# Window attention and a sign convolution on one core: the residuals' biases move from TensorE to GpSimd, the last norm's scaling from VectorE to ScalarE

## The reference

```python
x  = norm(x + window_mha(x, x) + sa_bf)            # windows of 8x8 tokens, 8 heads of 16
lo = norm(avg4(x) + window_mha(avg4(x)) + sa_bf)   # 16x16 points, the same weights
x  = norm(x + window_mha(x, patches of lo) + ca_bf)
x2 = norm(x + relu(x @ w1 + b1) @ w2 + ffn_b2)     # 128 -> 512 -> 128
y  = batchnorm(conv3x3(sign(x2), sign(weight)))    # statistics over all images
out = x2 + y
```

## Time and profile before

| | |
|---|---|
| three runs | 2511.85, 2498.77, 2510.22 us; median 2510.22 |
| profiled execution | 2505.16 us |
| its span, first to last instruction | 2503.3 us |
| mean granted clock of PE | 0.945 |
| busy: PE | 2163.3 us (86%) |
| busy: DVE | 1595.5 us (64%) |
| busy: ACT | 1368.4 us (55%) |
| busy: POOL | 943.7 us (38%) |
| DMA | 393.57 MB, 157 GB/s on average |

### The profile page before, as it was taken

One profiled execution on the slowest core, in us unless ns is written; L12 is line 12 of the kernel. 1 busy time (PEld: TensorE's weight loads), 2 busy tenths in 40 slices (PEclk: granted clock), 3 DMA queues, 4 the chain that ended last, 5 costly groups with the idle time before them and its releaser, 6 DMA issues.

```text
span 2503.3 us, 93142 instructions
## 1 busy us (share of the span) xinstructions
PE 2163.3 (86%) x39704; PEld 1734.1 (69%) x39704; DVE 1595.5 (64%) x5098; ACT 1368.4 (55%) x2531; POOL 943.7 (38%) x1080
## 2 busy tenths in 40 slices
PE   6997889998899979999799997999889998898860
PEld 4775777776677757777577776777667776676730
DVE  4886766776566756677466665676656764555535
ACT  3664555665466645666356654566555554554535
POOL 3443443443344433444334433444334443333300
PEclk9999999999899989999899998999999999999985
DMA  6775655655456645555355554555455553434429
GB/s 173 210 201 157 189 154 150 167 168 149 117 163 170 169 119 153 167 166 159 98 165 155 163 158 124 166 168 155 137 142 162 167 146 107 132 117 116 138 78 394
DMA packets 335102, 393.57 MB, mean 157 GB/s; under 512 B 40033, under 2 KB 239458, under 8 KB 334690
## 3 DMA queue, kind: packets, MB, share of 16 engines
q1 hardware_dynamic: 333842, 386.62, 53.0%
q10 hardware_dynamic: 848, 0.99, 0.1%
HBM read 208.29 MB, written 160.27 MB: 147 GB/s over the span
## 4 chain that ended last, share of the span: by engine, by line
PE 59%; DVE 29%; ACT 5%; issue 4%; DMA 1%; POOL 1%; SPq 0%; POOLq 0%; DVEq 0%; ACTq 0%
PE ps_hid L714 9%; PE ps_y L725 9%; PE ps_proj L577 6%; PE ps_o L662 6%; DVE onorm L951 5%; PE ps_s L643 4%; PE ps_hid L744 3%; PE ps_s L649 3%; PE ps_t L675 3%; DVE negmax L939 3%; DVE xn L993 3%; PE ps_max L633 3%; PE ps_y L694 2%; PE ps_y L681 2%; DVE stats L980 2%
## 5 line engine op out<-in xcount | busy, mean ns | idle before, releaser
L1097 POOL TENSOR_TENSOR prob_lo<-prob,prob_hi 128x512 f16<-128x512 f32 x528 | 611.0, 1157 | 915.1 <-ACT prob_hi L812 915.1
L811 ACT ACTIVATE prob<-ps_s 128x512 f32<-128x512 f32 x528 | 313.8, 594 | 401.2 <-PE ps_s L649 395.7
L946 DVE RECIPROCAL rden<-ps_o 128x8 f32<-128x8 f32 x528 | 107.4, 203 | 523.6 <-PE ps_o L662 522.4
L939 DVE TENSOR_REDUCE negmax<-ps_max 128x8 bf16<-128x512 f32 x528 | 360.5, 683 | 118.1 <-PE ps_max L633 113.7
L951 DVE TENSOR_TENSOR onorm<-ps_o,rden 64x128 f32<-64x128 f32 x1056 | 304.5, 288 | 25.6
L812 ACT ACTIVATE prob_hi<-ps_s 128x512 f16<-128x512 f32 x528 | 313.2, 593 | 0.0
L662 PE MATMUL ps_o<-vb,prob_hi 128*128 128x68 f16 x4224 | 294.7, 197 | 3.0 <-DVE onorm L951 2.9
L725 PEld LDWEIGHTS ps_y<-w_sb,hid 128*128 128x128 f32 x2048 | 266.8, 196 | 31.7 <-issue 26.8
L714 PE MATMUL ps_hid<-xf,w_sb 128*128 128x512 f32 x512 | 286.1, 641 | 3.0 <-ACT yconv L869 2.1
L725 PE MATMUL ps_y<-w_sb,hid 128*128 128x128 f32 x2048 | 277.8, 280 | 0.6 <-ACT hid L850 0.6
L662 PEld LDWEIGHTS ps_o<-vb,prob_hi 128*128 128x128 f16 x4224 | 261.6, 100 | 9.6 <-issue 5.3
(11 more groups left out here) (116 smaller groups left out, 3557.9 us busy)
## 6 DMA issues: line engine op xcount, KB each, us to landing
k_rows<-k_flat SPq DMA_DIRECT2D x256, 256.0 KB, 3.2
qs<-q_rows SPq DMA_DIRECT2D x512, 128.0 KB, 3.2
ks<-k_rows SPq DMA_DIRECT2D x128, 512.0 KB, 4.7
q_rows<-q_flat SPq DMA_DIRECT2D x128, 256.0 KB, 2.4
vb<-v_flat SPq DMA_DIRECT2D x128, 136.0 KB, 4.2
vb<-values_out SPq DMA_DIRECT2D x128, 136.0 KB, 2.9
xin<-in_x SPq DMA_DIRECT2D x64, 256.0 KB, 3.1
self_out<-xa SPq DMA_DIRECT2D x64, 256.0 KB, 3.4
```

The costliest lines, as they stand in the source:

```text
L811: activation(prob[:, pair_no(u, k) % 2, :], ps_s[:, :], ACT.Exp)
L939: v.tensor_reduce(negmax[:, pair_no(u, k) % 2, :], ps_max[:, :].rearrange("p (a t) -> p a t", t=TOK), AX.X, ALU.max, negate=True).then_inc ...
L1097: g.tensor_tensor(prob_lo[:, i, :], prob[:, i, :], prob_hi[:, i, :], ALU.subtract).then_inc(s_prob, 1)
```

## The change

The matmul L683, its weight `ones2`, `brow` and their setup are gone. The biases come in as three more columns of `columns_sb`, one value per channel, that is, per partition. POOL adds them to the tokens before PE's residual transposes: `add_bias` in place to a unit's tokens, once all its projections have read them, and `add_bias2` from xf into a new tile, xf_plus. PE waits for each. `apply2` moves to ACT: in place of subtracting the mean and multiplying by 1/sqrt, it multiplies and adds a shift, -mean/sqrt, that POOL makes with two more small operations per strip. The new stages have the due times bias and bias2; those of apply2 and all others stay. In the diff, the first `apply2_to` is in ACT's block, the second in DVE's.

```diff
-            project=6.2, stats=6.5, rstd=6.55, apply=6.9, spread=7.56, spread_out=7.66, store=8.0, pool=8.6)
+            project=6.2, stats=6.5, rstd=6.55, apply=6.9, spread=7.56, spread_out=7.66, store=8.0, pool=8.6, bias=-4.7)
...
-             spread_out=7.36, h0=8.2, relu0=8.4, h1=9.2, relu1=9.4, resid2=9.45, f0=9.47, h2=10.2, relu2=10.4,
+             spread_out=7.36, bias=-4.6, bias2=7.75, h0=8.2, relu0=8.4, h1=9.2, relu1=9.4, resid2=9.45, f0=9.47, h2=10.2, relu2=10.4,
...
-           rstd=3.45, apply=3.8, spread=4.68, spread_out=4.76, pad=5.2, expand=5.7, kk0=6.85, kk0_hi=7.05,
+           rstd=3.45, apply=3.8, spread=4.68, spread_out=4.76, bias=-5.5, pad=5.2, expand=5.7, kk0=6.85, kk0_hi=7.05,
...
+        add_sb = columns_sb[:, 8 + FB:11 + FB]
-        ones2 = sb("ones2", [128, 128], F16)
-        brow = sb("brow", [128, 3, PAIRS, C], F16)
+        neg_mean2 = sb("neg_mean2", [128, PAIRS])
+        shift2 = sb("shift2", [128, PAIRS])
+        xf_plus = sb("xf_plus", [128, SW])
...
         def _(sp):
-            sp.dma_start(brow_f[:, :], bias_rows).then_inc(s_bias, 16)
-            def setup_bias():
...
-            setup_bias()
...
-            def residual(ps, pairs, src, bias):
+            def residual(ps, pairs, src):
                 for p in range(pairs):
-                    mm(ps[:, C * p:C * p + C], src[:, C * p:C * p + C], ident[:, :], is_transpose=True,
-                       start=(p == 0), stop=False, skip_group_check=True)
-                return mm(ps[:, 0:C * pairs], ones2[:, :], brow[:, bias, 0:pairs, :].rearrange("p a c -> p (a c)"),
-                          start=False, stop=False, skip_group_check=True)
+                    done = mm(ps[:, C * p:C * p + C], src[:, C * p:C * p + C], ident[:, :], is_transpose=True,
+                              start=(p == 0), stop=False, skip_group_check=True)
+                return done
...
-                residual(ps_y, u.pairs, tokens_of(u), which(u)).then_inc(s_resid, 1)
+                pe.wait_ge(s_plus, plus_no["bias", u.seq, None])
+                residual(ps_y, u.pairs, tokens_of(u)).then_inc(s_resid, 1)
...
-                residual(ps_y2, PAIRS, xf[:, u.no % 2, :], 2)
+                pe.wait_ge(s_plus2, u.no + 1)
+                residual(ps_y2, PAIRS, xf_plus).then_inc(s_resid2, 1)
...
-            pe.wait_ge(s_brow, 16 * 2 * PAIRS)
-            pe.wait_ge(s_prep_v, 4)
+            pe.wait_ge(s_prep_v, 1)
...
+            def apply2_to(u):
+                if u.no:
+                    act.wait_ge(s_t, out_turn[u.no - 1])
+                act.wait_ge(s_rstd2, u.no + 1)
+                for p in range(PAIRS):
+                    activation(xn2[:, C * p:C * p + C], ps_y2[:, C * p:C * p + C], ACT.Identity, bias=shift2[:, p:p + 1],
+                               scale=rstd2[:, p:p + 1]).then_inc(s_xn2, 1)
...
-            def apply2_to(u):
-                if u.no:
-                    dve.wait_ge(s_t, out_turn[u.no - 1])
-                dve.wait_ge(s_rstd2, u.no + 1)
-                for p in range(PAIRS):
-                    v.tensor_scalar(xn2[:, C * p:C * p + C], ps_y2[:, C * p:C * p + C], mv2[:, p, 0:1],
-                                    rstd2[:, p:p + 1], ALU.subtract, ALU.mult).then_inc(s_xn2, 1)
...
+            def root_and_shift(var, var_eps, to, neg_mean, to_shift, pairs, count, mv_done, var_done, root_done, rstd_done):
+                pool.wait_ge(mv_done, count)
+                g.tensor_tensor(var_eps[:, 0:pairs], var[:, 0:pairs, 1], eps[:, 0:pairs], ALU.add)
+                g.tensor_scalar(neg_mean[:, 0:pairs], var[:, 0:pairs, 0], -1.0, None, ALU.mult).then_inc(var_done, 1)
+                pool.wait_ge(var_done, count)
+                g.tensor_tensor(to[:, 0:pairs], var_eps[:, 0:pairs], half_neg[:, 0:pairs], ALU.pow
+                                ).then_inc(root_done, 1)
+                pool.wait_ge(root_done, count)
+                g.tensor_tensor(to_shift[:, 0:pairs], neg_mean[:, 0:pairs], to[:, 0:pairs], ALU.mult
+                                ).then_inc(rstd_done, 1)
+
+            def add_bias(u):
+                pool.wait_ge(s_proj, proj_no["q" if u.kind == "cross" else "v", u.seq, None])
+                t, m = tokens_of(u), which(u)
+                g.tensor_scalar(t, t, add_sb[:, m:m + 1], None, ALU.add).then_inc(s_plus, 1)
+
+            def add_bias2(u):
+                pool.wait_ge(s_t_taken, turn_no["spread", u.seq, None])
+                if u.no:
+                    pool.wait_ge(s_resid2, u.no)
+                g.tensor_scalar(xf_plus[:, :], xf[:, u.no % 2, :], add_sb[:, 2:3], None, ALU.add).then_inc(s_plus2, 1)
```

More of the change, by code:

```diff
@@ L112, in stages_in_order, with attention_conv @@
     return [r[1:] for r in row]
-def attention_conv(nc, x, wq, wk, wv, wf, bias_rows, columns, w1, w2, convw, consts, out):
+def attention_conv(nc, x, wq, wk, wv, wf, columns, w1, w2, convw, consts, out):
     units = units_in_order()
@@ L161, in attention_conv @@
     resid_no = numbered("resid")
+    plus_no = numbered("bias")
     same_b = {}
@@ L210, in attention_conv @@
         w2_sb = sb("w2_sb", [128, FB, C])
-        columns_sb = sb("columns_sb", [128, 8 + FB])
+        columns_sb = sb("columns_sb", [128, 11 + FB])
         gain, shift = columns_sb[:, 0:3], columns_sb[:, 3:6]
         b1_sb, bn_sb = columns_sb[:, 6:6 + FB], columns_sb[:, 6 + FB:8 + FB]
+        add_sb = columns_sb[:, 8 + FB:11 + FB]
         consts_sb = sb("consts_sb", [128, 128 + 8])
@@ L217, in attention_conv @@
         identb = sb("identb", [128, 128], BF16)
-        ones2 = sb("ones2", [128, 128], F16)
-        brow = sb("brow", [128, 3, PAIRS, C], F16)
-        brow_f = sb("brow_f", [1, 3 * C])
-        brow_hi = sb("brow_hi", [1, 3 * C], F16)
-        brow_lo = sb("brow_lo", [1, 3 * C], F16)
         xin = sb("xin", [128, RING, SW])
@@ L300, in attention_conv @@
         s_setup = sem("s_setup")
-        s_bias = sem("s_bias")
-        s_brow = sem("s_brow")
         s_prep_v = sem("s_prep_v")
@@ L340, in attention_conv @@
         s_on = sem("s_on")
+        s_plus = sem("s_plus")
+        s_plus2 = sem("s_plus2")
         s_resid = sem("s_resid")
+        s_resid2 = sem("s_resid2")
         s_y = sem("s_y")
@@ L353, in attention_conv @@
         s_rstd2 = sem("s_rstd2")
+        s_root2 = sem("s_root2")
         s_xn2 = sem("s_xn2")
@@ L404, in _ @@
         def _(sp):
-            sp.dma_start(brow_f[:, :], bias_rows).then_inc(s_bias, 16)
             for to, src in setup_loads[0::2]:
                 sp.dma_start(to, src).then_inc(s_setup, 16)
-            def setup_bias():
-                sp.wait_ge(s_prep_v, 3)
-                for part, src in ((0, brow_hi), (1, brow_lo)):
-                    for p in range(PAIRS):
-                        sp.dma_start(brow[part:part + 1, :, p, :], src[:, :].rearrange("p (a c) -> p a c", a=3)
-                                     ).then_inc(s_brow, 16)
             def load(u):
@@ L878, in _ @@
                        ).then_inc(s_prep_a, 1)
-            act.wait_ge(s_prep_v, 4)
+            act.wait_ge(s_prep_v, 1)
             act.wait_ge(s_prep_g, 2)
             act.wait_ge(s_prep_a, 1)
-            walk({"q_hi": q_hi, "k_hi": k_hi, "v_hi": v_hi, "exp": exponentials, "turned": take_turned,
+            walk({"q_hi": q_hi, "apply2": apply2_to, "k_hi": k_hi, "v_hi": v_hi, "exp": exponentials, "turned": take_turned,
                   "spread_out": take_spread, "relu0": lambda u: take_hidden(u, 0),
@@ L1042, in conv_stats @@
                 v.bn_stats(ystats[:, strip, :], yconv[:, strip * SW:strip * SW + SW]).then_inc(s_ystats, 1)
[L1044 to L1053, removed]
             dve.wait_ge(s_setup, 16 * len(setup_loads))
             v.tensor_copy(identb[:, :], ident[:, :]).then_inc(s_prep_v, 1)
-            dve.wait_ge(s_prep_v, 4)
+            dve.wait_ge(s_prep_v, 1)
             dve.wait_ge(s_prep_g, 2)
             walk({"q_lo": q_lo, "k_lo": k_lo, "v_lo": v_lo, "rough": maxima, "weigh": normalise, "stats": stats_of,
-                  "apply": apply_to, "stats2": stats2_of, "apply2": apply2_to, "pool": pool, "make_low": make_low,
+                  "apply": apply_to, "stats2": stats2_of, "pool": pool, "make_low": make_low,
                   "pad": pad_low, "conv_stats": conv_stats, "kk0_lo": lambda u: kk_lo(u, 0),
@@ L1102, in rstd2_of @@
             def rstd2_of(u):
-                inv_sqrt(mv2, vareps2, rstd2, PAIRS, u.no + 1, s_mv2, s_var2, s_rstd2)
+                root_and_shift(mv2, vareps2, rstd2, neg_mean2, shift2, PAIRS, u.no + 1, s_mv2, s_var2, s_root2, s_rstd2)
             def expand(u):
@@ L1146, in _ @@
             walk({"prob_lo": split_prob, "rstd": rstd_of, "rstd2": rstd2_of, "expand": expand, "k_wrap": wrap_keys,
-                  "k_take": take_keys})
+                  "k_take": take_keys, "bias": add_bias, "bias2": add_bias2})
             pool.wait_ge(s_bn, 1)
@@ L1176 @@
```

(4 more changed lines are left out.)

## The result

The changed kernel takes 2535.09 us (median of 4 runs, 2530.08 to 2543.26), the one before 2511.03 (4 runs, 2498.77 to 2517.35). The ratio is 1.0105, with a 95% interval of 1.0058 to 1.0152: slower by 24 us. That is 26 us above the forecast's 2509 and outside its own range of 2492 to 2524; it lies 1 us inside the range of eight in ten (2484 to 2536), which reaches into the rivals. The profiled execution is 2530.08 us, of which the span is 2528.2 us, at a mean granted clock of 0.933 (before: 2503.3 and 0.945).

The account below looks back on a forecast made before the run. No engine alone was taken to bound the kernel: PE (59% of the chain) and DVE (29%) hand over to each other. Terms summed to -0.2 us; from the runs' median of 2510.22 it said 2509, own range 2492 to 2524.

Parts of the forecast that it names:

- (a): PE's bias matmuls L683 leave the chain: -27.1 us, two pieces of 0.21 us in a usual strip.
- (b): Setup: without the bias rows' small DMAs the first projection starts earlier, released by GpSimd's last memset; -1.7 us.
- Rival 4: L683's slot on PE is refilled by a wait for ScalarE's hid, bringing 6 us, not 27; 2530 us, chance 0.08.
- (c): The 200 bias additions on GpSimd take 0.6 us each, 120 us in all, hidden in its idle time; cost nothing.
- (d): Last norm's scaling through GpSimd and ScalarE: +12.2 in 33 usual strips, +4.1, -6.0 (coarse units), +8.3 in the last phase.
- Rivals 2 and 3: ScalarE's four scalings do not overlap: 2530 us, chance 0.15; or the scaling's detour costs nothing: 2467 us, chance 0.12.
- (e): PE's longer wait for the scaling halves the clock in 6 more strips at 1.6 us each: +10 us.
- rival 1: Longer PE gaps let the clock fall in most strips, 45 in place of 10; 2545 us, chance 0.15.

Follow-up runs that it names:

- e1: Changed kernel with the last norm's scaling back on VectorE, bias additions staying on GpSimd; 0.9903 of the kernel before, 2482.45 us against 2505.94.
- e8: e1 with each GpSimd addition replaced by a one-column operation and the last residual reading xf without bias; 0.9885 of the kernel before, 2477.33 us.
- e2: Kernel before with only the scaling moved to ScalarE and its shift made on GpSimd, biases still by PE's matmul; 1.0189 of before, 2552.15 us.
- e10: e3 with six more unread PE matmuls ahead of the last residual in the last phase's strips; 0.9904 of the kernel before, 2482.21 us.
- e9: e5 with six more unread PE matmuls ahead of the last residual in the last phase's strips; 0.9823 of the kernel before, 2460.78 us.
- e3: Changed kernel with four unread PE matmuls in the wait before turning the last norm's output, in 47 strips; 0.9963 of the kernel before, 2496.47 us.
- e6: Kernel before with e3's four unread PE matmuls in 47 strips; 0.9957 of the kernel before, 2493.24 us.
- e5: e1 with e3's four unread PE matmuls in 47 strips; 0.9832 of the kernel before.
- e7: e2 with e3's four unread PE matmuls in 47 strips; 1.0061 of the kernel before.
- e11: Changed kernel with -mean made by VectorE behind its statistics, one GpSimd operation less in the scaling's path; 1.0044 of the kernel before.

## Why the prediction failed

The sum was -0.2 us, and the profiled executions differ by 24.9. Step by step:

- **(a) The bias matmuls, -27.1.** Right in the usual strips. e1 has it alone: 0.46 us per short strip where two pieces of 0.21 were read from the chain, and 24 us in all with (b), of 28.8. Rival 4 (the slot is refilled), which left 6 of the 27, is refuted by it.
- **(b) Setup, -1.7.** Right in its mechanism: the first projection starts 1.78 us sooner, released by the memset. At the first L857 only 0.3 of it are left.
- **(c) The additions, 0.6 us each, hidden.** The duration is wrong, 1576 ns at 512 columns, above even the upper bound of 1.157; the bound assumed that one input can't cost more than two. The rule that they hide was right, as the 915 us of idle before prob_lo turned into 634; e8 puts what shows at 5 us, with some 7 either way. So the wrong duration cost the forecast little, by the room that GpSimd had.
- **(d) The detour, +0.37 a usual strip.** Right, within 0.1 us, in every part: start of the scaling +0.49 (forecast 0.42), 457 ns for one and (1.51 - 0.457) / 3 = 0.35 from start to start (0.36), k_lo +0.39 (0.37), short strips of e2 +0.37. Rivals 2 and 3 fall by this. In all, e10 less e9 puts it at 20 us, where the sum had 18.6. With (a) the short strips don't change: 32.37 against 32.38.
- **(e) The clock, 6 more strips, +10.** This step failed. Its mechanism, place and price were right (the wait before the turning; 1.6 us a strip forecast, 1.4 and 1.6 measured), and its count was not: 17 more, not 6. Before had 6 such strips where the prediction names 5, and the wait grew by 0.54 us, less than the 0.79 (0.2 and 0.59) from which the 6 was taken, so it is not an underrated wait that made them more. In the usual strips that makes 23 x 1.37 - 6 x 1.57 = +22 us. It is what rival 1 describes, which had named some 14 strips as the point from which it decides, and it got a chance of 0.15. e3 shows it by removing it: 23 long strips become none.

What lies between sum and result, then: +12 by (e), +2 as the short strips gained 0.01 and not 0.06 us each, +5 in the 13 other strips of the middle phase (-3.5 measured; 6.6 of (a), with +4.1 - 6.0 of (d), had -8.5), +6 in the last phase (+9.7, where 14 x 0.59 less some 4.8 of (a) had +3.5), +2.6 at the start (-0.3, where (b) and 1.2 of (a) had -2.9) and -2.8 in the tail (e1 has -2.9 there): 25. In the last phase the forecast had no clock term, and e10 against e3 shows that one was due there. Of the 13 strips with or beside a coarse unit I made no experiment, and what they gave back stays open; their sum also scatters, as e3 and e10, whose middle phases are the same program, have it at 601.4 and 611.2 us (after: 614.6).

I chose 6 strips because in most of before's strips such a wait did no harm. That was no evidence of slack: it said that 6 of 34 strips already were on the wrong side with a wait of 0.79 us, and nothing on how near the others stood. The Trainium skill (TensorE: Matmul & The Clock Gate, A second HAM failure mode: psum-queue depth-cycling) describes a kernel in which short idle times between groups of matmuls make the clock go to and fro, at a cost in throughput; these runs agree, and here one wait of some 1.3 us in each round of 32 goes with a fall in 23 of 34. What decides in a single strip isn't shown: of two neighbours with the same wait of 1.33 us one kept 2.4 GHz and one did not.

## What to carry to other kernels

Where PE waits in each round and the granted clock already falls behind some of these waits, cost a change that lengthens the wait with most rounds falling as one of its cases, and not with a few more: here 0.54 us more of waiting took them from 6 to 23 of 34. The 0.42 us of other work that left PE in each strip only paid for the detour itself. Before moving anything, try to fill that wait with matmuls that nobody reads: here this alone was worth 0.4% in the kernel before and 1.4% in the changed one. Here the work that went to an idle engine paid where nobody waited for it (the additions), and cost where it lay between a result and its reader through three engines (the scaling).

## What was not expected of the hardware

- GpSimd's addition of one value per partition to an f32 tile takes 1576 ns at 128x512 (1565 to 1588 in the 128 of L1091, so it isn't a wait in some of them that makes it long) and 927 ns at 128x256, so by these two points (1576 - 927) / 256 = 2.5 ns a column and 0.28 us fixed. The two-input subtraction of 128x512 takes 1158. The Trainium skill (GPSIMD Engine Reference, 3.1 Elementwise) gives 1.8 cycles an element at 1.2 GHz for a tight loop, 768 ns for 512 elements, and 2.6 where two inputs share a port, by which I estimate 1.11 us for 512. The second agrees with the trace's 1158 ns; the one-input addition, at 1576 ns, takes twice the first.
- More work on PE made the kernel faster in each of the four kernels it was added to, by 0.4, 0.7, 1.3 and 1.4% of before (e6, e5, e7, e3).
- An operation of 0.2 us on four columns moved the total by 0.6%, known to some 0.5% (e11); it stands in a serial chain that each strip passes, and the short strips alone lost 0.25 us each.
